# State added by unit products, centring as a product, and copies moved to ScalarE

## The reference

```
for i in range(6):
    x = attn_layer(shift_tokens(x), Wqkv[i], q_scale[i], k_scale[i], Wo[i]) + x
    x = ffn_layer(shift_tokens(x), ln_g[i], ln_b[i], W1[i], b1[i], W2[i], b2[i]) + x
# shift_tokens: features 64 to 127 come from the token before
# attn_layer: 16 heads of 64, unit norm and rotation of q and k,
#             attention in windows of 32 over this window and the last
# ffn_layer:  mu, var over the features;
#             ((x - mu) / sqrt(var + 1e-5) * g + bln) @ W1 + b1 -> a, gate;
#             (a * gelu(gate)) @ W2 + b2
```

## Time and profile before

| | us |
|---|---|
| median of 3 runs | 2174.64 |
| lowest and highest | 2171.32 and 2902.53 |
| the profiled execution | 2173.78 |
| its span | 2172.1 |

### The profile page before, as it was taken

One profiled execution on the slowest core, in us unless ns is written; L12 is line 12 of the kernel. 1 busy time (PEld: TensorE's weight loads), 2 busy tenths in 40 slices (PEclk: granted clock), 3 DMA queues, 4 the chain that ended last, 5 costly groups with the idle time before them and its releaser, 6 DMA issues.

```text
span 2172.1 us, 46645 instructions
## 1 busy us (share of the span) xinstructions
PE 1842.0 (85%) x19848; PEld 798.9 (37%) x19848; DVE 1672.5 (77%) x2643; ACT 847.3 (39%) x1340; POOL 1100.6 (51%) x822
## 2 busy tenths in 40 slices
...
DMA packets 91749, 131.40 MB, mean 60 GB/s; under 512 B 16242, under 2 KB 35856, under 8 KB 91536
## 3 DMA queue, kind: packets, MB, share of 16 engines
...
## 4 chain that ended last, share of the span: by engine, by line
PE 45%; DVE 32%; POOL 12%; issue 5%; ACT 3%; DMA 2%; SPq 1%; POOLq 0%; DVEq 0%; ACTq 0%
PE ps_z L1078 11%; DVE t L740 7%; PE ps_s L1055 5%; PE ps_r L1000 4%; POOL prob L503 4%; POOL k_hat L489 3%; PE ps_r L1106 3%; PE ps_r L1109 3%; DVE sinv L771 3%; PE ps_r L1113 3%; DVE prob L764 2%; DVE t L660 2%; DMA t<-t 2%; PE ps_z L889 2%; DVE pt L777 2%
## 5 line engine op out<-in xcount | busy, mean ns | idle before, releaser
L1000 PE MATMUL ps_r<-xs,w_qk_sb 128*128 128x512 f32 x768 | 438.4, 660 | 139.7 <-ACT sq L555 96.7
L740 DVE TENSOR_TENSOR t<-ps_r,rot 128x1024 f32<-128x1024 f32 x384 | 456.7, 1208 | 45.7 <-PE ps_r L1000 41.0
L493 POOL TENSOR_TENSOR prob<-prob,top 128x1024 f32<-128x1024 f32 x96 | 182.7, 1903 | 485.5 <-DVE top L768 485.2
L555 ACT ACTIVATE sq<-ps_r 128x512 f32<-128x512 f32 x384 | 229.7, 598 | 428.9 <-DVE t L740 427.2
L1078 PE MATMUL ps_z<-z,vo 128*128 128x512 f32 x768 | 356.3, 607 | 2.2 <-ACT z L577 2.2
L489 POOL TENSOR_TENSOR q_hat<-t 128x512 f32<-128x512 f32 x192 | 241.9, 1276 | 189.0 <-DMA t<-t 188.5
L489 POOL TENSOR_TENSOR k_hat<-t 128x512 f32<-128x512 f32 x192 | 244.5, 1289 | 31.3 <-DMA t<-t 28.2
L1000 PEld LDWEIGHTS ps_r<-xs,w_qk_sb 128*128 128x128 f32 x768 | 120.3, 194 | 375.8 <-ACT sq L555 267.0
L577 ACT ACTIVATE z<-ps_z 128x512 f32<-128x512 f32 x384 | 214.2, 605 | 94.4 <-PE ps_z L1071 94.2
L1071 PE MATMUL ps_z<-pt,xtk 32*128 32x512 f32 x1536 | 203.3, 644 | 41.2 <-DVE pt L777 35.3
L761 DVE TENSOR_TENSOR k_hat<-k_hat,ps_s 128x1024 f32<-128x1024 f32 x96 | 117.2, 1221 | 112.8 <-PE ps_s L1035 112.7
...
## 6 DMA issues: line engine op xcount, KB each, us to landing
t<-t SPq DMA_DIRECT2D x768, 128.0 KB, 2.1
...
z<-q_hat SPq DMA_DIRECT2D x128, 16.0 KB
...
```

The costliest lines, as they stand in the source:

```text
L493: nc.gpsimd.tensor_tensor(s, s, top[:, (TT * u + n) % P_SLOTS, :].unsqueeze(2).to_broadcast([P, HEADS, 2 * WIN]), ALU.subtract).then_inc(l ...
L555: nc.scalar.activation(sq[:, n % SQ_SLOTS, :], ps_r[n % 2][:, :], ACT.Square).then_inc(squared.sem, 1)
L740: nc.vector.tensor_tensor(t12[:, slot, :, :], ps_r[n % 2][:, :].unsqueeze(1).to_broadcast([P, 2, SEQ]), rot[:, n // PAIRS, :, :], ALU.mult ...
L1000: nc.tensor.matmul(ps_r[n % 2][:, :], w_qk_sb[:, n, :], xs[:, seq, WIN:WIN + SEQ], start=True, stop=True).then_inc(projected.sem, 1)
```

## The change

The state is no longer added by VectorE. Two products with the unit matrix (`add_rows`, 64 rows each) add it to the bank of `out` and, as x1, to the bank of `down`. `mean` multiplies by the unit matrix less 1/128, so that the centred x1 stands in the bank. `x1`, `center` and `new` are now copies out of PSUM on ScalarE, `new` with the bias. All four lists are reordered: `flip` 3, `mix` 3 and `project` 12 to 15 move into the next pass, `newton` 0 stands after `rotate` 11, `out` 3 comes before `hid` 0, and `score` 3 stands between `down` and `project` 1. `mask` has one more wait, on an earlier `flip`. The old lists of ScalarE and GpSimd are left out below.

```diff
@@ -71,41 +71,40 @@
 TENSOR_STEPS = [
-    ("out", 0, 2), ("project", 15, 1), ("nback", 0, 1), ("mean", 0, 3), ("xturn", 0, 1), ("spread", 0, 1),
-    ("sums", 3, 1), ("var", 0, 3), ("out", 1, 2), ("rows", 0, 3), ("spread", 1, 1), ("out", 2, 2), ("spread", 2, 1),
-    ("nturn", 1, 1), ("hid", 0, 3), ("spread", 3, 1), ("out", 3, 2), ("vo", 0, 2), ("hid", 1, 3), ("score", 0, 1),
-    ("hid", 2, 3), ("score", 1, 1), ("project", 0, 0), ("score", 2, 1), ("down", 0, 3), ("project", 1, 0),
-    ("xturn", 1, 1), ("project", 2, 0), ("score", 3, 1), ("project", 3, 0), ("mix", 0, 1), ("project", 4, 0),
+    ("mix", 3, 2), ("project", 12, 1), ("project", 13, 1), ("sums", 2, 1), ("out", 0, 2), ("project", 14, 1),
+    ("nback", 0, 1), ("project", 15, 1), ("spread", 0, 1), ("xturn", 0, 1), ("mean", 0, 3), ("out", 1, 2),
+    ("spread", 1, 1), ("var", 0, 3), ("sums", 3, 1), ("spread", 2, 1), ("out", 2, 2), ("rows", 0, 3),
+    ("spread", 3, 1), ("out", 3, 2), ("nturn", 1, 1), ("vo", 0, 2), ("hid", 0, 3), ("score", 0, 1), ("hid", 1, 3),
+    ("score", 1, 1), ("hid", 2, 3), ("score", 2, 1), ("project", 0, 0), ("xturn", 1, 1), ("down", 0, 3),
+    ("score", 3, 1), ("project", 1, 0), ("mix", 0, 1), ("project", 2, 0), ("project", 3, 0), ("project", 4, 0),
     ("project", 5, 0), ("mix", 1, 1), ("project", 6, 0), ("project", 7, 0), ("sums", 0, 0), ("project", 8, 0),
-    ("project", 9, 0), ("mix", 2, 1), ("project", 10, 0), ("sums", 1, 0), ("project", 11, 0), ("nturn", 0, 0),
-    ("project", 12, 0), ("mix", 3, 1), ("project", 13, 0), ("project", 14, 0), ("sums", 2, 0),
+    ("mix", 2, 1), ("project", 9, 0), ("sums", 1, 0), ("project", 10, 0), ("nturn", 0, 0), ("project", 11, 0),
 ]
 VECTOR_STEPS = [
-    ("newton", 0, 1), ("rotate", 13, 1), ("rotate", 14, 1), ("rotate", 15, 1), ("center", 0, 3), ("keyed", 0, 1),
-    ("rstd", 0, 3), ("keyed", 1, 1), ("gain", 0, 3), ("keyed", 2, 1), ("keyed", 3, 1), ("gated", 0, 3),
-    ("newton", 1, 1), ("gated", 1, 3), ("mask", 0, 1), ("max", 0, 1), ("gated", 2, 3), ("mask", 1, 1),
-    ("rotate", 0, 0), ("max", 1, 1), ("mask", 2, 1), ("max", 2, 1), ("new", 0, 3), ("psum", 0, 1), ("rotate", 1, 0),
-    ("x1", 0, 2), ("rotate", 2, 0), ("flip", 0, 1), ("psum", 1, 1), ("mask", 3, 1), ("rotate", 3, 0), ("max", 3, 1),
-    ("flip", 1, 1), ("rotate", 4, 0), ("rotate", 5, 0), ("psum", 2, 1), ("rotate", 6, 0), ("rotate", 7, 0),
-    ("flip", 2, 1), ("rotate", 8, 0), ("psum", 3, 1), ("rotate", 9, 0), ("rotate", 10, 0), ("flip", 3, 1),
-    ("rotate", 11, 0), ("rotate", 12, 0),
+    ("flip", 3, 2), ("rotate", 10, 1), ("rotate", 11, 1), ("newton", 0, 1), ("rotate", 12, 1), ("rotate", 13, 1),
+    ("rotate", 14, 1), ("rotate", 15, 1), ("keyed", 0, 1), ("keyed", 1, 1), ("rstd", 0, 3), ("keyed", 2, 1),
+    ("keyed", 3, 1), ("gain", 0, 3), ("newton", 1, 1), ("gated", 0, 3), ("mask", 0, 1), ("max", 0, 1),
+    ("gated", 1, 3), ("mask", 1, 1), ("max", 1, 1), ("gated", 2, 3), ("mask", 2, 1), ("psum", 0, 1), ("max", 2, 1),
+    ("rotate", 0, 0), ("flip", 0, 1), ("mask", 3, 1), ("rotate", 1, 0), ("max", 3, 1), ("psum", 1, 1),
+    ("rotate", 2, 0), ("rotate", 3, 0), ("flip", 1, 1), ("rotate", 4, 0), ("rotate", 5, 0), ("psum", 2, 1),
+    ("rotate", 6, 0), ("rotate", 7, 0), ("flip", 2, 1), ("psum", 3, 1), ("rotate", 8, 0), ("rotate", 9, 0),
 ]
 SCALAR_STEPS = [
...
+    ("xsq", 0, 3), ("xcopy", 0, 1), ("nevac", 1, 1), ("bias", 0, 3), ("vocopy", 0, 2), ("gelu", 0, 3), ("gelu", 1, 3),
+    ("gelu", 2, 3), ("exp", 0, 1), ("new", 0, 3), ("x1", 0, 2), ("xcopy", 1, 1), ("square", 0, 0), ("exp", 1, 1),
+    ("exp", 2, 1), ("zcopy", 0, 1), ("square", 1, 0), ("zcopy", 1, 1), ("square", 2, 0), ("square", 3, 0),
+    ("zcopy", 2, 1), ("zcopy", 3, 1), ("square", 4, 0), ("square", 5, 0), ("exp", 3, 1), ("zcopy", 4, 1),
+    ("zcopy", 5, 1), ("square", 6, 0), ("zcopy", 6, 1), ("zcopy", 7, 1), ("square", 7, 0), ("zcopy", 8, 1),
+    ("zcopy", 9, 1), ("square", 8, 0), ("nevac", 0, 0), ("square", 9, 0), ("zcopy", 10, 1), ("zcopy", 11, 1),
+    ("square", 10, 0), ("square", 11, 0), ("zcopy", 12, 1), ("zcopy", 13, 1), ("zcopy", 14, 1), ("zcopy", 15, 1),
+    ("square", 12, 0), ("square", 13, 0), ("nrows", 0, 0), ("square", 14, 0), ("square", 15, 0), ("center", 0, 2),
 ]
 GPSIMD_STEPS = [
...
+    ("lower", 1, 2), ("scale", 1, 2), ("pnorm", 0, 2), ("lower", 2, 2), ("scale", 2, 2), ("add", 0, 1),
+    ("lower", 3, 2), ("pnorm", 1, 2), ("add", 1, 1), ("scale", 3, 2), ("add", 2, 1), ("add", 3, 1), ("pnorm", 2, 2),
+    ("add", 4, 1), ("add", 5, 1), ("pnorm", 3, 2), ("add", 6, 1), ("add", 7, 1), ("add", 8, 1), ("add", 9, 1),
+    ("add", 10, 1), ("add", 11, 1), ("add", 12, 1), ("add", 13, 1), ("add", 14, 1), ("add", 15, 1), ("lower", 0, 1),
+    ("scale", 0, 1),
 ]
@@ -577,6 +577,15 @@
+                elif kind == "x1":
+                    act.wait_ge(attended.sem, attended.at(u, 3))
+                    act.wait_ge(x_new.sem, x_new.done(u - 1))
+                    nc.scalar.activation(x1s[0:64, 0:SEQ], ps_z[0:64, 0, :], ACT.Copy)
+                    nc.scalar.activation(x1s[64:P, 1:SEQ + 1], ps_z[64:P, 0, :], ACT.Copy).then_inc(x1_made.sem, 1)
+                elif kind == "center":
+                    act.wait_ge(xn_made.sem, xn_made.at(u - 1))
+                    act.wait_ge(mean_made.sem, mean_made.at(u))
+                    nc.scalar.activation(xc[:, :], ps_r[0][:, :], ACT.Copy).then_inc(xc_made.sem, 1)
@@ -586,6 +595,11 @@
+                elif kind == "new":
+                    act.wait_ge(down_made.sem, down_made.at(u))
+                    at = WIN + 1 if layer + 1 < DEPTH else WIN
+                    nc.scalar.activation(xs[0:64, seq, WIN:WIN + SEQ], ps_r[1][0:64, :], ACT.Identity, bias=vec[0:64, 8:9])
+                    nc.scalar.activation(xs[64:P, seq, at:at + SEQ], ps_r[1][64:P, :], ACT.Identity, bias=vec[64:P, 8:9]).then_inc(x_new.sem, 1)
@@ -619,6 +633,7 @@
+            nc.vector.tensor_scalar(centre_w[:, :], ident[:, :], -1.0 / P, None, ALU.add).then_inc(casts.sem, 1)
@@ -761,6 +776,7 @@
+                    dve.wait_ge(flipped.sem, flipped.at(u, n - 3) if n >= 3 else flipped.at(u - 1, n + 1))
@@ -776,16 +792,6 @@
-                elif kind == "x1":
-                    dve.wait_ge(attended.sem, attended.at(u, 3))
-                    dve.wait_ge(x_new.sem, x_new.done(u - 1))
-                    nc.vector.tensor_tensor(x1s[0:64, 0:SEQ], ps_z[0:64, 0, :], xs[0:64, seq, WIN:WIN + SEQ], ALU.add)
-                    nc.vector.tensor_tensor(x1s[64:P, 1:SEQ + 1], ps_z[64:P, 0, :], xs[64:P, seq, WIN + 1:WIN + 1 + SEQ], ALU.add).then_inc(x1_made.sem, 1)
-                elif kind == "center":
-                    dve.wait_ge(x1_made.sem, x1_made.at(u))
-                    dve.wait_ge(xn_made.sem, xn_made.at(u - 1))
-                    dve.wait_ge(mean_made.sem, mean_made.at(u))
-                    nc.vector.tensor_tensor(xc[:, :], x1s[:, 0:SEQ], ps_r[0][:, :], ALU.subtract).then_inc(xc_made.sem, 1)
@@ -804,14 +810,6 @@
-                elif kind == "new":
-                    dve.wait_ge(down_made.sem, down_made.at(u))
-                    at = WIN + 1 if layer + 1 < DEPTH else WIN
-                    nc.vector.scalar_tensor_tensor(out=xs[0:64, seq, WIN:WIN + SEQ], in0=ps_r[1][0:64, :], scalar=vec[0:64, 8:9], in1=x1s[0:64, 0:SEQ],
-                                                   op0=ALU.add, op1=ALU.add)
-                    nc.vector.scalar_tensor_tensor(out=xs[64:P, seq, at:at + SEQ], in0=ps_r[1][64:P, :], scalar=vec[64:P, 8:9],
-                                                   in1=x1s[64:P, 1:SEQ + 1], op0=ALU.add, op1=ALU.add).then_inc(x_new.sem, 1)
-
@@ -982,6 +980,11 @@
+            def add_rows(bank, src):
...
+                nc.tensor.matmul(bank[0:64, :], ident[0:64, 0:64], src[0:64, 0:SEQ], start=False, stop=True, skip_group_check=True)
+                return nc.tensor.matmul(bank[64:P, :], ident[64:P, 64:P], src[64:P, 1:SEQ + 1], start=False, stop=True, skip_group_check=True)
@@ -1075,7 +1078,9 @@
-                        ins = nc.tensor.matmul(ps_z[:, 0, :], vo[:, h, :], z[:, h, :], start=(h == 0), stop=(h == HEADS - 1))
+                        ins = nc.tensor.matmul(ps_z[:, 0, :], vo[:, h, :], z[:, h, :], start=(h == 0), stop=False, skip_group_check=True)
+                    if n == 3:
+                        ins = add_rows(ps_z[:, 0, :], xs[:, seq, WIN:WIN + 1 + SEQ])
@@ -1083,7 +1088,7 @@
-                    nc.tensor.matmul(ps_r[0][:, :], mean_w[:, :], x1s[:, 0:SEQ], start=True, stop=True).then_inc(mean_made.sem, 1)
+                    nc.tensor.matmul(ps_r[0][:, :], centre_w[:, :], x1s[:, 0:SEQ], start=True, stop=True).then_inc(mean_made.sem, 1)
@@ -1110,7 +1115,8 @@
-                        ins = nc.tensor.matmul(ps_r[1][:, :], w2_sb[0:rows, c, :], gate[0:rows, c, :], start=(c == 0), stop=(c == 2))
+                        ins = nc.tensor.matmul(ps_r[1][:, :], w2_sb[0:rows, c, :], gate[0:rows, c, :], start=(c == 0), stop=False, skip_group_check=True)
+                    ins = add_rows(ps_r[1], x1s)
```

(10 more changed lines are left out.)

15 lines of the change are left out of this document (5 added, 10 removed).

## The result

The changed kernel took 2140.99 us in the median (2132.2 to 2146.39, 4 runs) beside 2174.64 for the kernel before (2171.32 to 2187.66, 3 runs); one more run of the kernel before took 2902.53, fell into a slower state and is in no comparison here. The ratio is 0.985, 95% interval 0.981 to 0.989. So it gained 1.5%, where about 0.5% was forecast. The profiled execution took 2145.36 us, its span is 2143.6 against 2172.1.

A forecast was written before the change was run, and what follows sets the result against it. TensorE and VectorE were taken to come close to full together, neither alone. Span 2172.1, less 5 for some 23 passes, plus 2 for the tail, less 7 for bias, gave 2162; the median forecast was 2165, range 2090 to 2215.

The forecast's parts named there:

- the walk: A plain pass followed through the new lists from hid 0 with old durations: 71.9 us against 71.5, plus 0.4.
- the clock: Shorter TensorE gaps should make falls to the lower 1.2 GHz level rarer: 0.6 us off a pass.
- the walk's bias: The walk takes every handover whole where the trace overlaps neighbours by 0.07: 0.3 us off a pass, -7 in all.
- better-lists rival: VectorE's 4.2 us of waits shrink and the freed 3.6 us leave the pass: most likely 2115 us, chance 0.27.
- Stretch A: From hid 0 to the end of newton 0: 49.9 us, with VectorE standing 4.2 for exp 0, pnorm 1 and projections.
- The inverse root: newton 0 with its split on VectorE: 6.9 us again, as GpSimd's additions of this time come as before.
- Stretch B: From the end of newton 0 to the next hid 0: TensorE waits 1.5 us at project 14, then is never late.
- The pairs: Two pairs of unit products on TensorE, at down and out 3: 0.9 us each, halves in parallel, down's covered.
- the rival of dear pairs: The halves of a pair run one after the other, 1.8 us: 2200, or 2220 without cover at down; chance 0.16.
- ScalarE's queue: exp 1 stands behind new and may reach psum 1 late, by up to 1 us a pass: 2188, chance 0.08.
- The state's wait: TensorE's wait of 1.61 us for the new state at project 1 goes, as ScalarE writes it during score 3.
- The tail: One unit stands alone at the end; three pairs cost 2.7 us, shorter copies give back 1: +2.

The follow-up runs named there:

- e1: The new lists with the arithmetic of the kernel before (x1, center and new on VectorE, no unit products); 2163.25 us, ratio 0.996 to the kernel before.
- e15: The changed kernel with the first swap of a pass slowed to some 5 us and exp 0 made 1.1 us late; 2149.82 us, ratio 0.990.
- e16: The changed kernel run again without an edit, beside the runs with slowed swap or late exp 0; 2138.38 us, ratio 0.985 to the kernel before.
- e2: The new arithmetic with the lists of the kernel before; 2201.06 us, ratio 1.015 to the kernel before.
- e5: The changed kernel with score 3 put back behind project 1 in TensorE's list; 2174.62 us, ratio 1.003 to the kernel before.
- e7: The changed kernel with exp 1 and xcopy 1 ahead of new in ScalarE's list; 2142.66 us, ratio 0.988 to the kernel before.

## Why the prediction was wrong

The forecast for a pass was 0.4 us more by the walk, 0.6 less by the clock and 0.3 less for the walk's bias, so -0.5. It measured -1.73. The sign and the range held; the size did not, and the better-lists rival (2115) lay about as far on the other side. The walk itself was 2.1 us of a plain pass too long (71.9 against 69.8). The two small terms beside it, 0.9 together, brought the sum nearer, and the larger of them doesn't show as time (see the clock below): that part is luck.

**Stretch A, the step that failed.** These are the waits at `exp` 0 and at `add` 0 before `flip` 1. The walk put the table load of `exp` 0 on the path. In the new list `exp` 0 stands right behind `gelu` 2, and the load runs in the wait for `scale` 0; in the list of before `square` 0 stood between them, and the row that I priced it by the earlier trace rows is of that order. It also took 4.84 us from `rotate` 0 to its swap's landing, from a swap beside weight loads. Where `add` waited for a swap with no weight load beside it, it mostly started 2.65 to 2.8 after the end of the rotate: `add` 13 before, 24 of 24; `add` 12 after, 22 of 24; and `add` 0 itself in e1, where it waits in 22 of 24 passes, 2.73 to 2.82. So in the median pass `add` 0 starts at 19.87, set by GpSimd's own row, and `flip` 1 waits 0.35 in the pass shown and not 1.6. In 8 of the 24 passes of the changed kernel `add` 0 still waits, in four of them for a swap of 4.6 to 5.1 as the walk had it. Shown by e15 against e16: the two terms are worth 1.1 us in the median pass and 0.55 in the mean. The walk also kept the gelu's table load on the path; `gelu` 0 then ends 1.3 too late, which costs nothing, as `gated` 0 stands behind `newton` 1 (it ends at 3.95 in the walk and in the trace).

**The inverse root, the second term mis-sized.** From its first operation to the end of the split it lasts 6.3 us and not 6.9 (mean 6.34 after, 6.90 before), worth 0.6 (in e15, 42.96 to 49.32 where the walk has 43.0 to 49.9). The walk kept the old length because it expected the additions to land as before. e1 has 6.28 and e2 6.93, so the new lists do it, not the arithmetic. In the pass of before three operations ran long:

```profile
1366.93 1.09 DVE L696 TENSOR_SCALAR rnorm<-n_x 128x64 int32<-128x64 int32 x1
...
1368.28 1.31 DVE L702 TENSOR_TENSOR n_tmp<-rnorm 128x64 f32<-128x64 f32 x1
```

With the 1.30 of the earlier trace rows they make 3.7 us; in the pass of after it is 0.41, 1.23 and 1.22 (1070.15, 1072.64, 1073.90), 2.9. Additions ran for 3.9 us of that stretch before and for 3.2 after, as GpSimd there waits 2.00 for a swap. That reading is of one pass each, and no run moved an addition to try it. The prediction compared its 1.30 with a row of 0.21 that is another operation and lies within the additions of 1364.23 to 1367.96; the same operation undisturbed takes 0.22 (1371.49). The small operations of `rstd` gained too: two of them took 0.70 and 1.19 beside an addition before (1380.97, 1381.70) and 0.17 each after. Such operations are where I look for the rest of VectorE's fall: it is busy for 56.3 us in a pass, and the forecast's sign was 57.5.

**Stretch B.** 21.6 against 22.0, by the medians. TensorE waits 0.8 at `project` 14, the forecast had 1.5.

So the walk's 71.9 less 1.1, 0.6 and 0.4 is 69.8, the median measured (69.83). In the mean pass the forecast missed 1.2. Of it 0.55 is stretch A, by e15. e15, with the walk's terms of stretch A made real, is still 1.2 us shorter than before, not 0.5; the 0.7 between is what is left to the inverse root, stretch B and the clock's term, which no run takes apart.

**The clock.** TensorE's busy time rose by 1.34 in a pass, while two pairs are 2.0, so 0.66 came back; windows with a granted clock below 1.00 went from 10 of 21 to 4. The term of 0.6 holds as busy time. But the mean pass fell by 1.7 and the plain one shown by 1.9, so it doesn't show as time on top of the rest; whether TensorE's waits took it up stays open. The reason given, that shorter gaps make fewer falls, isn't borne out: counted from mark to mark the kernel before has falls in 9 passes at 8.13 us idle in a pass, e1 in 16 at 7.48 and e2 in 1 at 7.71. Their other runs agree, with a granted clock of 0.933 to 0.939 over the run in e1, 0.954 to 0.962 in e2 and 0.942 to 0.950 in the kernel before beside them. The new arithmetic doesn't settle it either, as e5 has falls in 15 passes with it. What decides their number stays open.

**The pairs.** 1.01 against 0.9 taken; 1.8 is out, and with it the rival of dear pairs. That the one of `down` is covered was right (0.23); the one of `out` 3 cost 1.38, which the sum had at 0.9.

**The copies.** `new` 1.38 for its two (taken 1.3), `x1` 1.2 (1.15), `center` 0.60 (0.6): right. ScalarE's queue did no harm: VectorE waits 0.04 a pass for exps, and e7 changes nothing.

**The state's wait.** It is gone, as forecast, but its worth was hidden in the walk's total: in e5 a wait of 1.48 comes back and the pass is 1.8 longer, 0.7 of it busy time at a lower clock.

**The tail.** +2.5 against +2. **The fill and the first block** were left at 0; the later start of 8.9 in the profile goes with the lower clock of that execution, and e16 has 0.6.
